# Scattering edge records from 128 partitions in place of 125

## The reference

```python
edge_index = stack([src, dst])
x = layernorm(x + L0(x, edge_index, edge_attr_40, ...))     # gates, then 4 attention layers per source node
x = layernorm(x + L1(x, edge_index))                        # 5 steps of h = 0.2*(A_norm h) + 0.8*x
x = layernorm(x + L2(x, edge_weight, src, dst))             # 10 steps of f = 0.9*(A_w f) + 0.1*feat
x = layernorm(x + L3(x, edge_weight1, ..., src, dst, edge_type_8))
#   L3: msg = h2[src, rel_type] * norm;  relu(segment_sum(msg, dst) + bias2)
```

## Time and profile before

| | |
|---|---|
| Time before, median of 3 runs | 10487.99 us (10485.22 to 10488.97) |
| Span of the profiled execution, first to last instruction | 10489.7 us |
| PE busy | 7567.5 us, 72% |
| DVE busy | 5964.3 us, 57% |
| POOL busy | 4653.2 us, 44% |
| DMA packets | 2230019, 1959.97 MB |
| Scatters of the first order (L456), POOL busy | 800, 943.0 us |
| Scatters of the second order (L1877), POOL busy | 800, 949.8 us |

### The profile page before, as it was taken

The page is one execution under the profiler, slowest core; times in us unless marked ns, Lnnn a source line. Parts: engine busy times, 40 slices in busy tenths (PEclk is TensorE's granted clock), DMA queues, the critical chain, the costliest instruction groups (busy, mean ns, idle before and its releaser), DMA issues. The chain is left out here.

```text
span 10489.7 us, 325649 instructions
## 1 busy us (share of the span) xinstructions
PE 7567.5 (72%) x107650; PEld 6145.6 (59%) x107651; DVE 5964.3 (57%) x19883; ACT 3702.8 (35%) x13000; POOL 4653.2 (44%) x6218
## 2 busy tenths in 40 slices
PE   2999975666665867994996798599578788843332
PEld 1777754555555756993995798499434344433332
DVE  6444457777775778996997899699700100011111
ACT  3222215666662324772663576277300000100000
POOL 0677760000004653551552455155266566346665
PEclk9999998767777988996997899699799999755555
DMA  8222226777777976992993798399488899411112
GB/s 316 59 59 59 60 48 199 220 220 220 219 220 215 310 229 193 261 247 76 260 261 107 214 261 227 96 261 263 120 333 340 314 361 365 159 32 18 18 18 18
DMA packets 2230019, 1959.97 MB, mean 187 GB/s; under 512 B 1473446, under 2 KB 1872326, under 8 KB 2191078
## 3 DMA queue, kind: packets, MB, share of 16 engines
q1 hardware_dynamic: 1872642, 1712.86, 53.1%
q10 hardware_dynamic: 252000, 173.83, 5.5%
q0 software_dynamic: 105216, 71.18, 3.7%
HBM read 1481.79 MB, written 473.73 MB: 186 GB/s over the span
## 5 line engine op out<-in xcount | busy, mean ns | idle before, releaser
L1615 POOL TENSOR_TENSOR s_rest<-s_msg 128x196 f32<-128x196 f32 x1488 | 762.5, 512 | 1920.6 <-ACT s_msg L1597 1868.8
L1207 PE MATMUL s_gotd<-m_table_d,s_hot 128*128 x17856 | 1362.9, 205 | 203.2 <-DMA s_hot<-OHT 193.5
L1597 ACT ACTIVATE s_msg<-s_gotd,s_es 128x49 f32<-128x49 f32 x5952 | 1304.6, 303 | 48.4
L1207 PE MATMUL s_gotq<-m_table_s,s_hot 128*128 x17856 | 1279.3, 185 | 7.5 <-issue 7.5
L1207 PEld LDWEIGHTS s_gotd<-m_table_d,s_hot 128*128 128x128 bf16 x17856 | 989.0, 96 | 288.8 <-DMA s_hot<-OHT 195.0
L1877 POOL DMA_INDIRECT REC<-m_sums x800 | 949.8, 1187 | 354.1 <-issue 347.2
L456 POOL DMA_INDIRECT REC<-rec,place x800 | 943.0, 1179 | 329.7 <-issue 214.9
L2140 POOL DMA_INDIRECT l_row<-H,l_rec x816 | 784.2, 961 | 628.7 <-DMA l_rec<-REC 303.8
L1910 PE MATMUL p_acc<-p_row,p_feats 128*64 128x512 f32 (+1 forms) x4032 | 899.8, 570 | 164.1 <-DMA p_row<-ADJ 161.9
L1648 DVE TENSOR_REDUCE s_tops<-s_mt 128x512 f32 (+1 forms) x1488 | 1013.6, 681 | 6.3 <-PE s_mt L1558 6.3
L1207 PEld LDWEIGHTS s_gotq<-m_table_s,s_hot 128*128 128x128 bf16 x17856 | 992.2, 97 | 6.1 <-issue 6.1
(11 more groups left out here) (418 smaller groups left out, 19927.9 us busy)
## 6 DMA issues: line engine op xcount, KB each, us to landing
s_hot<-OHT SPq DMA_DIRECT2D x1488, 384.0 KB
p_row<-ADJ SPq DMA_DIRECT2D x288, 1600.0 KB
ADJ<-a_acc SPq DMA_DIRECT2D x1488, 128.0 KB
s_rec<-REC SPq DMA_DIRECT2D x1488, 98.0 KB
OHT<-a_turned ACTq DMA_DIRECT2D x372, 384.0 KB
g_hot<-OHT SPq DMA_DIRECT2D x372, 384.0 KB
REC<-fill SPq DMA_DIRECT2D x124, 624.0 KB, 10.2
g_rec<-REC SPq DMA_DIRECT2D x372, 108.0 KB
```

The lines of the kernel that those rows point to most:

```text
L1207: last = nc.tensor.matmul(out, hot, table[k][:, bass.ds(at, w)], start=(k == 0), stop=(k == 2))
L1597: last = nc.scalar.activation(msg[:, b % KEPT, j], gotd[b % KEPT][:, j, SW:2 * SW], ACT.Copy, scale=es[:, b % 2, j:j + 1])
L1615: nc.gpsimd.tensor_tensor(rest[:, b % KEPT].rearrange("p g w -> p (g w)"), msg[:, b % KEPT].rearrange("p g w -> p (g w)"), upper(msg[:, b ...
```

## The change

Both kinds of scatter take 128 partitions in place of 125. Partitions 125, 126 and 127 carry no edge. Their places are written once by `iota` and name rows behind the end of the table, a row of its own for each, so that no two of one scatter meet. Both tables grow by `ASIDE` = 300 rows for this, and everything that reads or fills them goes by a view of the rows before. `rec` and `place` get 128 partitions, and what writes to them by edges is cut to `[0:EP]`; the same holds for the tiles of the second scatter. One wait is added on DVE (for the iota, before the first step), and one on POOL in each call of `propagate` and in the first scatter's block. The scatter lines L456 and L1877 themselves are not edited: they take whatever partitions their tiles have.

```diff
+ASIDE = (P - EP) * 2 * CHUNK
...
-        rec = sb("rec", [EP, RSLOTS, RT, RW], F32)
+        rec = sb("rec", [P, RSLOTS, RT, RW], F32)
...
-        place = sb("place", [EP, RSLOTS, RT], I32)
+        place = sb("place", [P, RSLOTS, RT], I32)
...
                 nc.gpsimd.memset(rec[:], 0.0).then_inc(s_zero, 1)
                 nc.gpsimd.memset(hidden[:], 1.0).then_inc(s_zero, 1)
+
+                nc.gpsimd.iota(place[:].rearrange("p b t -> p (b t)"), [[P - EP, RSLOTS * RT]], base=T * P - EP,
+                               channel_multiplier=1).then_inc(s_aside, 1)
+                pool.wait_ge(s_aside, 1)
...
                 dve.wait_ge(s_zero, 1)
+                dve.wait_ge(s_aside, 1)
...
-    mem["REC"] = dram("REC", [T * P, RW])
-    mem["REC_G"] = mem["REC"].rearrange("(g p r) w -> g p (r w)", p=P, r=G)
-    mem["REC2"] = dram("REC2", [T2 * P, META - 2])
-    mem["REC2_G"] = mem["REC2"].rearrange("(g p r) w -> g p (r w)", p=P, r=G)
+    mem["REC"] = dram("REC", [T * P + ASIDE, RW])
+    mem["REC_G"] = mem["REC"][0:T * P].rearrange("(g p r) w -> g p (r w)", p=P, r=G)
+    mem["REC2"] = dram("REC2", [T2 * P + ASIDE, META - 2])
+    mem["REC2_G"] = mem["REC2"][0:T2 * P].rearrange("(g p r) w -> g p (r w)", p=P, r=G)
...
-        moved = nodes(mem["sums"][0:EP])
+        moved = nodes(mem["sums"][:])
...
-                    nc.gpsimd.dma_start(numbers_of[b], mem["META"][:, cols]).then_inc(s_chunk[b], 16)
-                    nc.gpsimd.dma_start(places_of[b], mem["PLACE2"][:, cols]).then_inc(s_chunk[b], 16)
-
+                    nc.gpsimd.dma_start(numbers_of[b][0:EP], mem["META"][:, cols]).then_inc(s_chunk[b], 16)
+                    nc.gpsimd.dma_start(places_of[b][0:EP], mem["PLACE2"][:, cols]).then_inc(s_chunk[b], 16)
+
+                for b in range(2):
+                    nc.gpsimd.iota(places_of[b], [[P - EP, CHUNK]], base=T2 * P - EP + b * (P - EP) * CHUNK,
+                                   channel_multiplier=1).then_inc(s_aside, 1)
+                pool.wait_ge(s_aside, 2)
                 fetch(0)
```

More of the change, by code:

```diff
@@ L181, in _ @@
                 sp.wait_ge(s_fill, 3)
-                whole = mem["REC"].rearrange("(p k r) w -> p k r w", p=P, r=FR)
+                whole = mem["REC"][0:T * P].rearrange("(p k r) w -> p k r w", p=P, r=FR)
                 for k in range(T // FR):
@@ L185, in _ @@
                 sp.wait_ge(s_fill, 5)
-                whole2 = mem["REC2"].rearrange("(p k r) w -> p k r w", p=P, k=8)
+                whole2 = mem["REC2"][0:T2 * P].rearrange("(p k r) w -> p k r w", p=P, k=8)
                 for k in range(8):
@@ L396, in sort_edges @@
         s_zero = sem("s_zero")
+        s_aside = sem("s_aside")
         s_ea = [sem(f"s_ea{b}") for b in range(RSLOTS)]
@@ L434, in attributes @@
                             sp.wait_ge(s_scat[b], 16 * RT * i)
-                        sp.dma_start(rec[:, b, :, 0:RBF], ea[:, bass.ds((RSLOTS * i + b) * RT, RT)]
+                        sp.dma_start(rec[0:EP, b, :, 0:RBF], ea[:, bass.ds((RSLOTS * i + b) * RT, RT)]
                                      ).then_inc(s_ea[b], 16)
@@ L559, in ranks @@
                         dve.wait_ge(s_scat[slot], loaded(n, slot, 16 * RT, RSLOTS) - 16 * RT)
-                    v.tensor_copy(rec[:, slot, :, CW:GATES], meta[:, cols]).then_inc(s_meta, 1)
+                    v.tensor_copy(rec[0:EP, slot, :, CW:GATES], meta[:, cols]).then_inc(s_meta, 1)
                     dve.wait_ge(s_rank, n + 1)
@@ L579, in ranks @@
                     ch.step(v.tensor_tensor(pa[:], pa[:], pb[:], ALU.bitwise_or))
-                    ch.step(v.tensor_tensor(place[:, slot], pa[:], pc[:], ALU.bitwise_or))
+                    ch.step(v.tensor_tensor(place[0:EP, slot], pa[:], pc[:], ALU.bitwise_or))
                     dve.sem_inc(s_place, 1)
@@ L586, in weigh @@
                     dve.wait_ge(s_gate, n + 1)
-                    v.tensor_tensor(rec[:, slot, :, GATES:RW], gate[:],
+                    v.tensor_tensor(rec[0:EP, slot, :, GATES:RW], gate[:],
                                     meta[:, bass.ds(n * RT, RT), 0:1].to_broadcast([EP, RT, H]), ALU.mult
@@ L1830, in propagate @@
             room.sem(n) for n in ("s_used", "s_f", "s_dve", "s_deg", "s_root", "s_x", "s_up", "s_back", "s_sum"))
-        s_tick = room.sem("s_tick")
+        s_tick, s_aside = room.sem("s_tick"), room.sem("s_aside")
         s_chunk = [room.sem(f"s_chunk{b}") for b in range(2)]
         s_second = [room.sem(f"s_second{b}") for b in range(2)]
-        moved = nodes(mem["sums"][0:EP])
+        moved = nodes(mem["sums"][:])
         numbers_of = [moved[:, b * CHUNK * META:(b + 1) * CHUNK * META].rearrange("p (t w) -> p t w", w=META)
```

## The result

| | median | runs |
|---|---|---|
| Before | 10488.48 us | 4 (10485.22 to 10489.45) |
| After | 11475.63 us | 4 (11467.68 to 11484.95) |
| After / before | 1.0942 | 95% interval 1.0927 to 1.0958 |

The kernel became 9.4% slower, 987 us. I had predicted 10447 us and a range up to 10487, so the time lies far outside it, and on the other side.

A forecast was written before the change was run, and what follows sets the result against it. PE was taken to bound the first scatter, the DMA engines `propagate`. Savings of 38.7 (DMA load) and 1.9 us (last eight scatters) made 40.6 off the 10489.7 span, 10449.1; with the median 1.7 below the span, 10447 us, range 10426 to 10487.

The forecast's parts named there:

- the load on the DMA engines: `propagate`: fewer descriptors per ring save 0.052 us per scatter while DMA is the limit, 744 scatters, 38.7 us.
- the last eight: First scatter's block: only the last step's eight scatters are not hidden behind PE; 8 x 0.233 = 1.9 us saved.
- C: Both scatters: a scatter becomes longer on POOL, with 16 rings of real rows; 10573 us at 1.30 us each; chance 0.04.
- A: Row loads in `propagate`: small writes, not descriptors, are the scatter's cost, and become 128 from 125; 10488 us; chance 0.12.
- B: `propagate`: a scatter stays at 1.177 us on POOL, so the second call gains at most 1 us; 10473 us; chance 0.07.
- the stages without a scatter stay as they are: Adjacency, gates, attention layers and L3's own work meet no scatter and stay unchanged, unless the longer tables move something.
- The number of packets: Software queue: 32 packets per scatter with 128 partitions, like the gather, in place of 64.
- my 0.944: POOL's time per new scatter in us, taken from the 128-row gather, against 1.177 before.
- the main term: Relief of the DMA engines in `propagate`: 38.7 us saved, with 20.8 and 57.3 as ends.
- 13.7 and 38.7 in all: DMA relief in us: 264 x 0.052 = 13.7 in the first `propagate` call, 38.7 over both calls.
- my ends of 0.028 and 0.077: Saving per scatter in us: 0.077 if all 0.118 goes with descriptor number, 0.028 if only the recorded packet time does.
- my division of the 0.118 us: A scatter costs each ring 0.118 us in `propagate`; 17/26 of it goes if it follows the number of descriptors.

The follow-up runs named there:

- f1: Kernel after, but first scatter as before (125 partitions) and a 306-column memset behind each `propagate` scatter, 1.50 us apart; 10442.52 us, ratio 0.9954 to before.
- g1: As f1, plus a 262-column memset behind each L3 gather, gathers 1.456 us apart; 10428.32 us, ratio 0.9952 to the kernel before.
- g3: As g1, with memsets of 204 columns, gathers 1.41 us apart; 10406.91 us in one run, against 10478.63 for the kernel before.
- h1: The kernel of g3 timed once more, in 5 runs; 10417.48 us, ratio 0.9931 to the kernel before.
- e1: Kernel before, both scatters cut to partitions 0 to 111 (16 rings with 7 rows each, no rows aside); 11418.35 us.
- e2: Kernel after, with the rows aside spread 32 rows apart in place of adjacent; 11430.28 us.
- e4: Kernel before, both scatters cut to partitions 0 to 99 (10 rings with 10 rows each); 11463.69 us.
- e3: Kernel after, with a 12-column memset and a wait behind each scatter in `propagate`; 11244.70 us.

## Why the prediction was wrong

**The step that failed** is in the part on the load on the DMA engines: "That POOL issues faster changes nothing in the sum, since the number of scatters stays." I also counted POOL's shorter scatter as hidden, with a price only for the last eight. I had thought of POOL's time as a supply that could only help by being shorter. The runs show it as a demand on the other engines: with POOL's starts 1.50 us apart a strip takes 3.0 us on the mean, at 1.40 us 4.6, at 1.27 us with nothing between 39.2. The 26 descriptors per ring of the 125-partition form looked like mere cost, and they held the scatters 1.48 us apart. The change removed that brake.

**No rival had it.** C, the only one on the slower side, had the scatter become longer on POOL; it became shorter. A and B are out, too: 969 ns is not 1177, and f1 shows the relief. The premise that the stages without a scatter stay as they are held: the two in the table moved by 4 and 6 us. L3's own gathers had the trouble before and after. Chances of 0.08 on slower and a range up to 10487 came from rows that all held POOL at 1.48 us apart while others worked. The one stage that had shown faster indirect DMAs next to other engines' work was L3, and I took from it only the 944 ns. The sum there would have been a warning: 816 gathers at 1.25 us are 1020 us and not the 1197 between first and last start.

**What held.** The number of packets: 14905 packets for 466 scatters are 32 each, as for the gathers, against 64 before:

```profile
q0 software_dynamic: 14905, 24.82, 9.2%
...
REC<-rec,place POOLq DMA_INDIRECT x466
```

By the Trainium skill, "DMA: Bandwidth & Descriptors", section "Why a DMA increments its semaphore by 16 and not by 1", 128 rows go to 16 engines and 125 to 5. These rows agree: at 32 packets per scatter, 24.82 MB are 53300 bytes each, which is 128 x 416 and 64, and the 1100 bytes of idle descriptors are gone. POOL's time was 0.967 and 0.969 us, 0.02 above my 0.944. And the main term, measured where the pace is held (f1): the first call ends 15.8 us earlier than before (8161.44 and 8145.65), the second 44.7 us (9042.29 and 8997.57). I had 13.7 and 38.7 in all. Per scatter that is 44.7 / 744 = 0.060 us, between my ends of 0.028 and 0.077 and near the 0.052 that I took. From the first scatter to ACT's last copy it is 1410.6 us in f1 and 1401.1 to 1410.9 in g1, g3 and h1, which have the same `propagate`, against 1454.2 before: 43 to 53 us. So the relief is of the size that I gave, and it is worth 0.5%; it could not be seen behind the 981 us. That it follows the number of descriptors, as my division of the 0.118 us has it, was not tested by itself.

**What stays open** is what the engines share. The waits say "issue", which names nothing. Two ways out are closed by rows. It is not a lock between DVE and POOL: in 7800:7900 DVE has no instruction at all, and PE has 36. And it is hardly the loading of the program. The Trainium skill, "Runtime: NRT & Kernel Launch", section "Instruction fetch mechanics", says that a sequencer fetches its instructions by DMA in blocks of 256; by that rule a slow fetch would show as one pause in 256 instructions. Here every one of PE's 71 instructions in 100 us comes late (the DMA engines are busy to 0.18 there). The trace points the same way: its queues for instructions move two packets from 7800 to 7900, and none from 8040 to 8090, where PE still starts only 19 matmuls. That PE and in the end POOL are held at multiples of 0.70 us speaks for one resource that the indirect DMAs take up, by their descriptors or their completions, and that hands out turns. That is argued and not shown: no run separated these two, and none was made with completions taken away, since something must wait for the data. All executions were also recorded by the profiler, so no run tells whether the writing of its records has a part in it.

## What to carry to other kernels

Before making an operation shorter, ask what its length had held back: an engine off the critical path that repeats one kind of instruction hundreds of times has a pace, and the other engines may live by it. Where POOL issues indirect DMAs in a long row beside other work, look at the spacing of their starts. In `propagate` 1.46 to 1.50 us was the least that left PE alone, and a memset that made the spacing so long was faster than none; in L3, where PE has less to do, 1.41 us gave the shortest stage of the spacings tried. In a profile the sign is "issue" in the waits of an engine that has its data, with a low DMA share, and a stage of POOL's that takes longer than its instructions' number times their spacing.

## What the runs showed of the hardware

- With indirect DMAs 1.24 to 1.29 us apart and nothing between, PE started an instruction every 1.40 us (39.2 us for 28 of them, in after, e1, e2 and e4), its granted clock fell to 0.50 (1.2 GHz), and after some 180 to 340 of them in a call POOL was held to 1.39 to 1.40 us itself for most of the rest.
- It did not matter whether a scatter of the second kind had 100, 112 or 128 rows, or 10 or 16 rings with rows (14 or 15 matmuls in 40 us each). The 125-row form, 1.18 us long, left PE 167 matmuls in 40 us; the 128-row form with pauses to 1.50 us did as well (3.0 us for 14 matmuls), so the length is what set it apart.
- A scatter of 125 rows costs 64 packets and 1.177 us on POOL, one of 128 rows 32 packets and 0.967 us, one of 100 rows 0.980 and one of 112 rows 0.932 us.
- A memset of 12 columns and a wait behind an indirect DMA cost next to nothing in the median spacing (1.28 us in e3, against 1.27): they fit into the 0.30 us that lie between two of them anyway.
